# Fewer chunks made on chip, 16-bit gate and up inputs, and a last output added from PSUM, in an RWKV and quantised-FFN kernel

## The reference, cut to what matters

```python
x = x + tanh(g_xattn[0]) * xattn(layernorm(x), ctx, ctx, w, u)   # decayed sums over all positions, both ways
x = x + tanh(g_ffn[0])   * ffn(layernorm(x), clip_x, clip_down, w_gate, w_up, w_down)

def act_fake_quant(x, clip):            # one scale for the whole tensor
    scale = sigmoid(clip) * max(abs(x)) / 127
    return clip(round(x / scale), -128, 127) * scale
def ffn(x, ...):
    xq   = act_fake_quant(x, clip_x[0])                       # needs the peak of all of x first
    gate = einsum('bsh,ih->bsi', xq, weight_fake_quant(w_gate))   # i = 704, h = 256
    up   = einsum('bsh,ih->bsi', xq, weight_fake_quant(w_up))
    h    = act_fake_quant(silu(gate) * up, clip_down[0])      # needs the peak of all of h first
    return einsum('bsi,hi->bsh', h, weight_fake_quant(w_down))
```

## Time and profile before

| | us |
|---|---|
| median of 3 runs | 212.69 (212.09 to 212.9) |
| the profiled execution, its own time | 211.43 |
| span of the profiled execution, first to last instruction | 209.7 |
| busy DVE / PE / ACT / POOL | 166.8 / 172.9 / 157.4 / 138.7 |
| mean granted TensorE clock | 0.949 of full speed |

### The profile page before, as it was taken

One profiled execution on the slowest core, in us unless ns is written; L12 is line 12 of the kernel. 1 busy time (PEld: TensorE's weight loads), 2 busy tenths in 40 slices (PEclk: granted clock), 3 DMA queues, 4 the chain that ended last, 5 costly groups with the idle time before them and its releaser, 6 DMA issues.

```text
span 209.7 us, 3447 instructions
## 1 busy us (share of the span) xinstructions
PE 172.9 (82%) x1146; PEld 125.8 (60%) x1146; DVE 166.8 (80%) x352; ACT 157.4 (75%) x242; POOL 138.7 (66%) x163
## 2 busy tenths in 40 slices
PE   4489996989899989988137987969889997789990
PEld 4456536989899989978126662324334432467780
DVE  0769586365755949999969968999799999889994
ACT  3459698737698699599879996958978891899910
POOL 3355223638869979986788852848897664058983
PEclk9969997899999999999855899999999999999998
DMA  3999999999999998500000000000000000025555
GB/s 89 331 375 348 349 328 292 296 283 297 278 292 319 243 250 216 159 28 2 0 0 0 0 3 2 0 0 0 0 3 0 0 0 2 3 76 171 171 185 200
DMA packets 43328, 29.31 MB, mean 140 GB/s; under 512 B 2224, under 2 KB 43056, under 8 KB 43312
## 3 DMA queue, kind: packets, MB, share of 16 engines
q1 hardware_dynamic: 42896, 28.58, 47.7%
q10 hardware_dynamic: 416, 0.52, 0.7%
HBM read 24.65 MB, written 4.46 MB: 139 GB/s over the span
## 4 chain that ended last, share of the span: by engine, by line
PE 34%; DVE 27%; ACT 17%; DMA 10%; issue 7%; POOL 3%; SPq 1%; DVEq 0%; ACTq 0%
PE ps L1019 10%; PE ps L1123 9%; DMA hidden<-lag_w 6%; PE ps L1159 5%; PE ps L1003 5%; DVE hidden L893 4%; DMA hidden<-in_ctx 4%; ACT hidden L551 3%; ACT z_t L702 2%; DVE hidden L911 2%; PE ps L1050 2%; DVE h_peaks L922 2%; ACT hidden L627 2%; ACT silu_out L681 2%; DVE z_t L964 2%
## 5 line engine op out<-in xcount | busy, mean ns | idle before, releaser
L1019 PE MATMUL ps<-hidden 128*128 128x128 f32 (+1 forms) x512 | 60.4, 280 | 6.0 <-DVE hidden L723 2.5
L1019 PEld LDWEIGHTS ps<-hidden 128*128 128x128 f32 x512 | 59.5, 196 | 7.4 <-issue 3.3
L922 DVE TENSOR_REDUCE h_peaks<-hidden (+2 forms) x24 | 26.0, 1122 | 2.0 <-POOL hidden L476 1.3
L418 POOL TENSOR_TENSOR x_all<-x_all,silu_out 128x512 f32<-128x512 f32 x15 | 22.9, 1542 | 6.3 <-DVE silu_out L792 6.3
L780 DVE SCALAR_TENSOR_TENSOR h_space<-z_t,ps 128x256 f32<-128x256 f32 x32 | 19.1, 598 | 8.6 <-PE ps L1019 8.2
L1159 PE MATMUL ps<-wdT,z_t 128*128 128x256 bf16 x192 | 22.6, 272 | 2.5 <-DVE z_t L964 2.3
L681 ACT ACTIVATE silu_out<-ps,mix_scale 128x1024 f32<-128x1024 f32 (+1 forms) x18 | 18.4, 1020 | 5.8 <-PE ps L1123 3.4
L1159 PEld LDWEIGHTS ps<-wdT,z_t 128*128 128x128 bf16 x192 | 17.6, 97 | 7.7 <-DVE z_t L964 2.9
L1043 PE MATMUL ps<-ident,hidden 128*128 128x128 f32 x64 | 11.6, 342 | 10.0 <-POOL hidden L457 8.5
L792 DVE SCALAR_TENSOR_TENSOR silu_out<-ps,small,silu_out 128x256 f32<-128x256 f32 x32 | 15.1, 476 | 5.5 <-ACT silu_out L532 3.4
L521 ACT ACTIVATE z_t<-x_all,mr,nr 128x256 f32<-128x256 f32 x32 | 16.4, 588 | 3.6 <-POOL mr L380 3.6
(11 more groups left out here) (116 smaller groups left out, 374.0 us busy)
## 6 DMA issues: line engine op xcount, KB each, us to landing
hidden<-lag_w SPq DMA_DIRECT2D x26, 512.0 KB, 7.3
x_all<-in_x SPq DMA_DIRECT2D x8, 512.0 KB, 8.9
hidden<-in_ctx SPq DMA_DIRECT2D x8, 512.0 KB, 9.1
out<-x_all SPq DMA_DIRECT2D x15, 256.0 KB, 2.1
xq<-in_L_ffn_w_down SPq DMA_DIRECT2D x1, 704.0 KB, 6.1
xq<-in_L_ffn_w_gate SPq DMA_DIRECT2D x1, 640.0 KB, 6.9
h_space<-in_L_ffn_w_up SPq DMA_DIRECT2D x1, 640.0 KB, 6.2
out<-x_all ACTq DMA_DIRECT2D x1, 256.0 KB, 2.4
```

What stands on the lines that cost most here:

```text
L418: nc.gpsimd.tensor_tensor(xs, xs, mixed[:, m % 2, :, :].rearrange("p c b -> p b c"), ALU.add).then_inc(s["x1_done"], 1)
L922: nc.vector.tensor_reduce(h_peaks[:, bass.ds(KA * b + k, 1)], hidden[:, bass.ds(b * HB + k * BT, cols)], AX.X, ALU.max, apply_absolute_val ...
L1019: last = nc.tensor.matmul(ps[:, j % BANKS, c * 2 * SEQS:end * 2 * SEQS], lag_tile(j)[:, c, :], ekp[:, (j * CK + c) * 2 * SEQS:(j * CK + en ...
```

## The change

In the lag stage `MADE` loses chunks 22, 26 and 30, which are then loaded; the third `turn_weights` moves behind chunk 31, `exp_clips` and `sigmoid_clips` move to earlier pairs. In the gate and up stage the 8-bit numbers in `x8` go: groups are rounded to 16-bit numbers in the place of their bf16 form and then clipped and cast there by DVE. Groups 0 and 1 are rounded half by DVE, half by ACT; group 2 by ACT, 3 by DVE, 4 to 7 by POOL, which then casts none. DVE's loop over blocks is written out, with the two casts of blocks 2 and 3 in it and two peaks moved. In the down stage the first rounded pieces and their casts are divided otherwise, groups 2 and 3 of block 0 go through `pair_int`, DVE rounds one piece of block 1, and the last output is scaled in PSUM and added from there.

```diff
-    MADE = 10, 14, 18, 22, 26, 30
+    MADE = 10, 14, 18
...
+        X_BY_POOL = [4, 5, 6, 7]
+        def x_int(n):
+            return whole_x(n // 2)[:, n % 2, :, :].bitcast(I16)
+        def x_normed(n):
+            return z_t[:, :, n * 512:(n + 1) * 512]
...
-        CASTS = [(0, 0, 0, 2), (0, 0, 2, KI), (0, 0, KI, KA)] + [(0, i, 0, KI) for i in range(1, OUTS)] \
-            + [c for b in range(1, BLOCKS) for c in [(b, 0, KI, KA)] + [(b, i, 0, KI) for i in range(OUTS)]]
+        CASTS = [(0, 0, 0, 2), (0, 0, 2, 4), (0, 0, 4, KI), (0, 0, KI, KA), (0, 1, 0, KI), (0, 2, 0, KI), (1, 0, KI, KA), (0, 3, 0, KI)] \
+            + [c for b in range(1, BLOCKS) for c in ([(b, 0, KI, KA)] if b > 1 else []) + [(b, i, 0, KI) for i in range(OUTS)]]
...
+        QUANTS = [(0, 0, 1, 4, KI), (0, 0, OUTS, KI, KA), (0, 1, 2, 0, KI), (0, 2, 3, 0, KI), (0, 3, 4, 0, KI),
+                  (1, 0, 1, 0, KI), (1, 1, 2, 0, KI), (1, 2, 4, 0, KI)] \
+            + [q for b in range(2, BLOCKS) for q in [(b, 0, OUTS, KI, KA), (b, 0, 2, 0, KI), (b, 2, 4, 0, KI)]]
+        BY_DVE = [0, 1, CASTS.index((1, 0, KI, KA))]
...
POOL:
-            def cast_x(b):
-                for n in (2 * b, 2 * b + 1):
-                    pool.wait_ge(s["x8_done"], n + 1)
-                    nc.gpsimd.tensor_copy(whole_x(b)[:, n % 2, :, :], x8[:, n, :, :]).then_inc(s["xq_cast"], 1)
+            def quantise_x(n):
+                pool.wait_ge(s["x_int_own"], 3)
+                pool.wait_ge(s["x_int_act"], 2)
+                nc.gpsimd.tensor_scalar(x_int(n), x_normed(n), S["inv_x"], 1.0, ALU.mult, ALU.mult).then_inc(s["x_int_pool"], 1)
-            cast_x(1)
+            for n in X_BY_POOL[0:2]:
+                quantise_x(n)
             for b in range(BLOCKS):
                 for i in range(EVEN):
                     multiply(b, i)
-                if b + 2 < BLOCKS:
-                    cast_x(b + 2)
+                if b == 0:
+                    for n in X_BY_POOL[2:]:
+                        quantise_x(n)
...
ACT:
-            cast_first()
+            act.wait_ge(s["inv_x_done"], 1)
+            for n in range(2):
+                nc.scalar.activation(x_int(n)[:, 1, :], x_normed(n)[:, 1, :], ACT.Copy, scale=S["inv_x"]).then_inc(s["x_int_act"], 1)
+            act.wait_ge(s["z_kept"], 3)
+            nc.scalar.activation(x_int(2), x_normed(2), ACT.Copy, scale=S["inv_x"]).then_inc(s["x_int_act"], 1)
...
DVE:
-            for n in range(2, GROUPS):
-                quantise_x(n)
+            def cast(dst):
+                nc.vector.tensor_scalar(dst, dst.bitcast(I16), QMAX, -QMAX - 1.0, ALU.min, ALU.max).then_inc(s["xq_done"], 1)
+            for n in range(2):
+                quantise_x(n, 0)
+                dve.wait_ge(s["x_int_own"], n + 1)
+                cast(whole_x(0)[:, n, 0, :])
+                dve.wait_ge(s["x_int_act"], n + 1)
+                cast(whole_x(0)[:, n, 1, :])
             nc.vector.tensor_scalar(mix_scale[:, :, :], w_scale[:, :, :], S["s_x"], None, ALU.mult).then_inc(s["scale_x"], 1)
+            quantise_x(3)
+            dve.wait_ge(s["x_int_own"], 3)
+            dve.wait_ge(s["x_int_act"], 3)
+            cast(whole_x(1))
...
+            for b in range(BLOCKS):
+                if b > 0:
+                    peak(b - 1, 4)
                 multiply(b, 1)
-                peak(b, 0)
                 peak(b, 1)
+                if b == 0:
+                    dve.wait_ge(s["x_int_pool"], 2)
+                    cast(whole_x(2))
+                else:
+                    peak(b, 0)
                 multiply(b, 3)
+                if b == 0:
+                    peak(b, 0)
+                if b == 1:
+                    dve.wait_ge(s["x_int_pool"], 4)
+                    cast(whole_x(3))
                 peak(b, 3)
                 multiply(b, 5)
                 peak(b, 2)
                 peak(b, 5)
-            hidden_block(0, True)
-            with dve.Fori(1, BLOCKS) as b:
-                hidden_block(b, False)
...
             def evict(n):
-                nc.vector.scalar_tensor_tensor(ffn[n // 4 % 2][:, n % 4, :], ps[:, n % 8, :], S["out_scale"], flat_row,
+                dst = ps[:, n % 8, :] if n in dve_sums else ffn[n // 4 % 2][:, n % 4, :]
+                nc.vector.scalar_tensor_tensor(dst, ps[:, n % 8, :], S["out_scale"], flat_row, ALU.mult, ALU.mult) \
             def add_rest(n):
-                nc.vector.tensor_tensor(xs, xs, ffn[n // 4 % 2][:, n % 4, :], ALU.add).then_inc(s["dve_sum_done"], 1)
+                nc.vector.tensor_tensor(xs, xs, ps[:, n % 8, :], ALU.add).then_inc(s["dve_sum_done"], 1)
...
-                while cast < needed(min(n + 2, SUMS - 1)):
+                while cast < needed(min(n + (1 if n < 2 else 2), SUMS - 1)):
+                    if cast == BY_DVE[2]:
+                        quantise_h(*CASTS[cast])
...
PE:
-                if j in (14, 23, 30):
-                    turn_weights((14, 23, 30).index(j))
+                if j in (14, 23):
+                    turn_weights((14, 23).index(j))
+            turn_weights(2)
```

More of the change, by code:

```diff
@@ L640, in _ @@
                     cast_weights((5, 9, 13).index(m))
-                if m == 12:
+                if m == 9:
                     exp_clips()
@@ L954, in cast_h @@
                 src = dst.bitcast(I16)
-                if n < 2:
-                    dve.wait_ge(s["h_int_own"], n + 1)
-                elif k == KI:
-                    dve.wait_ge(s["h_int"], QUANTS.index((b, 0, OUTS, KI)) + 1)
-                elif b == 0:
-                    dve.wait_ge(s["h_int"], QUANTS.index((b, i, i + 1, 0)) + 1)
-                else:
-                    dve.wait_ge(s["h_int"], QUANTS.index((b, i - i % 2, i - i % 2 + 2, 0)) + 1)
+                if n in BY_DVE:
+                    dve.wait_ge(s["h_int_own"], BY_DVE.index(n) + 1)
+                else:
+                    done = [m for m, (at_, first, last, k0, k1) in enumerate(QUANTS)
+                            if at_ == b and (k0, k1) == (k, end) and first <= i < last]
+                    dve.wait_ge(s["h_int"], done[0] + 1)
+                if k < KI and b * OUTS + i >= 2:
                     src = pair_int[(b * OUTS + i) // 2 % 2][:, :, i % 2 * 256:(i % 2 + 1) * 256]
```

78 lines of the change are left out of this document (30 added, 48 removed).

## The result

The changed kernel takes 204.51 us (median of 4 runs, 204.12 to 205.33), the kernel before on the same chip 212.66 (212.09 to 212.9): a ratio of 0.9626, 95% interval 0.959 to 0.9662, 8.15 us less. The forecast was 208.8 with a range of 207.3 to 212.0, a gain of 3.85. The sign was right; the gain is twice the forecast and lies outside the range.

What follows compares the result with a forecast made beforehand. DVE was taken to bound the late lag stage; PE, ACT and DVE were nearly balanced in gate and up. Gains 0.65 + 3.0 - 0.35 + 0.55 = 3.85 off 212.69 gave 208.8 us, range 207.3 to 212.0.

Steps and rivals of the forecast that it cites:

- the 0.65 of the lag stage: Lag stage: without three made chunks DVE's mix starts 0.75 sooner, denominator 31 comes 0.65 us sooner; bounds 0 and 1.5.
- Loads: Lag stage: three more 512 KB loads, 290 GB/s wanted, cost zero; they decide only under some 225 GB/s.
- Rival 3: Lag stage: loads fall behind under 225 GB/s and chunk 31 sets the end; 210.1 us, chance 0.04.
- Gate and up, the start: DVE's first product 5.9 us after the reciprocal instead of 9.5, 3.6 sooner; POOL's rounding of a group at 1.1.
- the 4.7 without waits: Gate and up: last peak 4.7 us sooner if DVE never waits, from the earlier start and written-out blocks of 9.6.
- the 1.7 for waits: Gate and up: DVE's waits from POOL, between none and one late cast, leaving 3.0 us gain for the stage.
- A late cast: Gate and up: DVE's cast of block 2 or 3 meets a POOL multiply and waits about 2.4 us.
- Rival 2: Gate and up: POOL becomes the bound, from about 1.95 us a rounding; slower, 213.6 us, chance 0.08.
- Rival 4: Lag stage and gate and up: no cast waits and the lag stage gives 1.2; 207.3 us, chance 0.08.
- Down: Down stage: first eviction sooner, but more DVE casts and a new collision with POOL; 0.35 us lost, bounds 1.0 lost, 0.8 won.
- Last output: Kernel's end: last addition from PSUM takes 0.72 instead of 1.33 us; 0.55 gained.
- The loop written out: Gate and up: a block takes DVE 9.6 us instead of 10.04 without addresses from registers.

## Why the prediction was wrong, by its own steps

**The step that failed: "The mix after it and the work behind it start 0.75 sooner. Then DVE works through without a gap", and with it the 0.65 of the lag stage.** The term was 0.65 with bounds 0 and 1.5. Seven profiles of kernels with six made chunks, and no other edit ahead of the normalising stage, end their reciprocal at 126.25 to 128.53, mean 127.65; eight with three made chunks at 123.68 to 125.79, mean 124.78. The stage is worth 2.9 us. One execution's end varies by 2 us, and PE's waits for loads ahead of 64 us by 1.6 to 3.8, so single profiles can't tell this.

A piece of the stage repeats far better: from the start of DVE's reduction over the third weight matrix to denominator 31. Its first row before, then after:

```profile
79.32 1.74 DVE L731 TENSOR_REDUCE small<-xq 128x2 f32<-128x1536 f32 x1
78.46 1.74 DVE L737 TENSOR_REDUCE small<-xq 128x2 f32<-128x1536 f32 x1
```

| | us |
|---|---|
| six made chunks, six of the seven profiles | 20.51 to 20.56 |
| gate and up alone, the seventh | 20.23 |
| three made chunks, eight profiles | 18.04 to 18.06 |
| the same, POOL's instructions back | 20.18 |
| the same, ACT's exponentials back | 18.24 |
| six made chunks, the diagonals on ACT | 18.90 |

So 2.5 of the 2.9 lie in this piece, and the two rows shown above account for them: they hid 2.74 us (0.83 + 2.67 against 0.17 + 0.59), and with three made chunks they take 0.17 and 0.59 in all eight profiles. A `down_diag` took a mean of 1315 ns for 128 elements, where the denominator's instruction takes 0.59 us for 256. The rows lie at 81.09 to 84.71, in a window in which DVE is busy 9.57 of 12.00 us: a DVE instruction that waits for the shared port counts as busy, so there is no gap to see. The stretch behind them, 13.69 of 14.00, was read rightly: DVE is the bound there, and so the time reaches the end. The prediction had the lock and wrote that "only the eight 8-bit roundings and a few casts in the down stage could collide"; it never asked which DVE instructions of the lag stage meet POOL's. Putting work back on POOL that nobody reads made them long again, and moving the two diagonals off DVE gave 1.6 of the 2.5 with POOL's work untouched. ACT's exponentials, the path that the prediction did follow, are worth 0.19 in this piece; what they are worth ahead of it (the lead of 0.75) no run here can tell from the 2 us by which executions vary.

The Trainium skill's "SBUF — State Buffer", section "Who interferes with whom", says that `tensor_scalar` can take both ports and is then blocked for the whole of a GpSimd instruction that began first. The rows agree down to two elements a partition: 0.83 for 0.17.

**Loads.** As forecast: 293 GB/s from 74 to 86, no wait of PE for a lag tile behind 64 in this profile. Four of the other kernels with three made chunks have one of 0.16 to 0.79 near 69 or 70, which none with six has. Rival 3 did not come.

**Gate and up, the start.** Right in each row: 5.9 and 1.1.

**Gate and up, the waits.** The stage gave 4.37, the 4.7 without waits less 0.3; the 1.7 for waits was wrong. A late cast was a matter of which of two instructions starts first. In every profile of this stage without added work the order is the same one (DVE by 0.04), so it is no toss that comes out anew. That it fell on this side, by 0.04, was luck. POOL's chain, though, has as little slack as the prediction said (within 0.3 us): 2.2 us more there cost 3.7 in the stage. Rival 2 was a real mechanism with the wrong price for POOL. Rival 4 (no late cast and more from the lag stage) is what came, and more than it took; its own sum was off too, since 0.55 + 0.65 more than 3.85 makes 207.6 and not 207.3.

**A gain that the prediction did not have: PE's wait.** DVE's late first product let PE stand for 2.22 us, and behind that the clock fell in some executions, for 1.3 to 1.5 us at the end of the stage. The change removes the wait. The profile of the kernel before happened to be an execution without the fall, so no row of it could show this; that it lay 1.26 under its own median was a hint, and I added the difference to the forecast instead of asking where it comes from. A hint only: the lag stage alone moves an execution by as much. The sum is now 2.9 + 4.4, less 0.4 for the end (30.94 against 30.53), and, since about half of the profiles with the wait have the fall, 0.7 for it: 7.6, against 8.15 measured (7.2 to 8.7 by the interval of the ratio). How often the kernel before falls was not counted beyond these six profiles; the last part is an estimate.

**Down.** -0.35 forecast, -0.1 in the traces, with the collision at the place named. **Last output.** The addition is 0.64 shorter as forecast, but worth nothing that a measurement shows. The two terms were 0.2 together and came to -0.4 at the span's end. POOL's last sum, 0.08 behind, is now as late as the addition; whether it or the stores behind both set the end stays open.

**The loop written out.** Booked at 1.3 over three blocks; alone 0.8 with an interval from 1.7 to nothing. That it pays more together with the rest, with the other engines at nearly the same pitch, is a guess that no run tests.

## What to carry to other kernels

Before calling an engine the bound, compare each of its short instructions with its size: one that takes 1.3 us for 128 elements is waiting, and the busy share hides it. Work on POOL costs DVE time even if nobody waits for it, and moving a DVE `tensor_scalar` to ACT, or out of POOL's way, can be worth more than its own work: here 1.6 us for two that take 0.59. When the profiled execution lies clearly under the median, the kernel may have a cost that this profile doesn't show; a second profile of the same kernel is the cheapest experiment.

## What the runs showed of the hardware

- The port shared by DVE and POOL catches instructions of 2, 6 and 128 elements too: 0.83 for 0.17 us; 1.47 for 0.17 (of six elements, 69.30 after, and its shortest, in the profile of gate and up alone); 2.67 for 0.59 (two of 128).
- A wait of PE of 2.22 us, after dense work, is followed by the lower clock in three of six profiles of this stage and not in the others; waits of 2.11, 2.61, 5.02 and 7.67 were followed by it in the one profile of each (with the 7.67 it fell inside the wait). "TensorE: Matmul & The Clock Gate" of the Trainium skill, section "What's actually happening", says that the number of matmuls at the lower clock at a kernel's start differs between runs of the same kernel; these rows show the like in the middle of one.
- The stage from reciprocal to reciprocal repeats to 0.02 us (47.52 to 47.54 in eight profiles), while the lag stage ahead of it, with its loads, varies by 2. Single stages can be compared far more finely than whole times.
